# Eleven tiles that outlive a block of a three-block fused kernel

## The chip, the core and the metric

The kernel runs on one core of a Trainium2 chip. The metric is the time of one execution on the device in microseconds. Five engines work from queues of their own: TensorE (PE, its weight loads shown as PEld), VectorE (DVE), ScalarE (ACT), GpSimd (POOL) and SyncE (SP), which here issues all DMA transfers. They are ordered by semaphores alone.

## What is computed

Four layers on x and a context ctx, both 32 x 128 x 512 float32. Their sizes are batch B = 32, T = 128 tokens, D = 512.

```
L0: x = LayerNorm(x + Wo . attention(x Wq, ctx Wk, ctx Wv))       # 32 heads, 8 key/value heads of 16
L1: g, theta = conv(x); phi = conv(ctx); y = softmax(phi theta) g; wy = Wz y + bz
    x = x + gamma * (wy - mean) / sqrt(var + eps) + beta           # mean and var over batch and features
L2: a recurrent mixing layer (32 heads of 16, state from ctx) and its feed-forward part
L3: x = x + cproj(attention(LN(x) q_w, ctx k_w, ctx v_w))          # 16 heads of 32, masked
    x = x + proj(gelu(fc(LN(x))))                                  # 512 -> 2048 -> 512
```

The statistics of L1 run over the whole batch, so L2 can't begin for any row before L1 is done for all.

## The kernel before

`program` runs four functions one after the other, each with tiles, semaphores and an `nc.Block()` of its own. A block ends when all five engines have ended their programs in it.

- `phase_a` (tiles a_...): L0 and the part of L1 up to wy, in 16 turns of two batch rows. It leaves x (`dram["x1"]`), wy (`dram["wy"]`) and the transposed context (`dram["cT"]`) in DRAM.
- `phase_norm` (n_...): the statistics of L1, a few tiny operations that end in the tile `norm`.
- `phase_b` (b_...): L2 in 16 turns of two batch rows. In the idle places of its first and last turns it also computes L3's keys and values for all eight groups of four rows (`unit`, matmuls on L1338 for a K unit and L1343 for a V unit; results through L1492 and L1684 to `dram["k"]` and `dram["v"]`). The units of groups 0 to 2 are side 0 (first turns), the others side 1 (last turns). Their weights and contexts lie in tiles that are not otherwise in use then: for side 0, k_w in `Wfk`, v_w in `Wfr`, the context of even groups in `Wfv` and of odd groups in `Wo`. The result of the layer goes to `dram["x4"]`.
- `phase_c` (c_...): L3 in eight turns of four rows.

Within a block every engine runs the same hand-written table of steps, three static turns ahead of and four behind a loop in a and b (one ahead, one behind in c). SyncE's program is a list of waits and transfers in order; a transfer behind a wait on SyncE can't be issued until that wait is over. Where a step does not exist in a static turn, the engines count its semaphores up instead.

How the blocks begin:

- `phase_b`, SyncE, L1076 to L1096: `vec`, `ident`, `heads`, `parity`, `state` (these five count into `loaded_w`); then `x1g` and `wyg`, the rows of x and wy for the first turn (L1033, L1034, `y_loaded`); then `load_kv(0)` (L1052): k_w, the two halves of group 0's context, v_w, `rows_c` (the bias of v), the halves of group 1's context; then two small states and the weights of L2.
- `phase_b`, TensorE waits for `loaded_w` and for `consts` to reach 6 (L1163), then begins the first units, which wait for `kv_weights` and `groups_loaded`. VectorE waits for `loaded_w`, then sets half, A, two v_pad and heads_wide and copies heads (L1499 to L1505, six counts of `consts`). GpSimd builds its masks, then waits for `consts`. ScalarE normalises wy (L1373), GpSimd adds x (L1709), VectorE takes statistics (L1511).
- `phase_c`, SyncE, L1953 to L1964: four loads of x rows, `ident`, `vec`, q_w, `load_k`, `load_mask`, `load_v`, `rows` (two biases), cproj_w, fc_w (4 MB), proj_w (4 MB). `loaded_k` counts ident and vec, `loaded_att` q_w, rows and cproj_w.
- `phase_c`: VectorE takes the statistics of four rows (L2106 to L2111), GpSimd the reciprocal roots (L2184), VectorE whitens (L2115), and TensorE transposes (L1994), then q (L2000), scores (L2024) and so on. GpSimd's program begins with a wait for the whole of `loaded_att` (L2180); TensorE's and ScalarE's with a wait for `loaded_k`.

How they end: in `phase_a` SyncE's last two turns store the last rows (L334, L338) and wait for them; in `phase_b` the last unit is stored (L1066), then the last two rows (L1044), and SyncE waits for all.

Of the kernel before, what the change touches and what calls it, by code (L numbers as in the profile page):

```python
# [19 lines left out]
P = 128  # L20
# [120 lines left out]
def phase_a(nc, dram, stats):  # L141
# [34 lines left out]
    with ExitStack() as ctx:  # L176
# [44 lines left out]
        cT_stored = sig("cT_stored", 16)  # L221
# [63 lines left out]
        def _(sp):  # L285
# [101 lines left out]
            sp.wait_ge(*cT_stored(N - 1, 16))  # L387
# [335 lines left out]
def phase_b(nc, dram, norm):  # L723
# [89 lines left out]
    with ExitStack() as ctx:  # L813
# [13 lines left out]
        vec = sb("vec", [P, dram["vecs"].shape[1]])  # L827
        ident, heads, parity = sb("ident", [P, P]), sb("heads", [P, HC]), sb("parity", [P, 2])
# [8 lines left out]
        x1g, wyg, x2 = sb("x1g", [P, G, D]), sb("wyg", [P, G, D]), sb("x2", [P, G, D])  # L837
# [85 lines left out]
        def groups_loaded(side, group):  # L923
            nth, buffer = divmod(group - sides[side][0][3][1], 2)
            return kv_context[buffer].sem, 32 * (nth + 1 + (len(range(buffer, NEARLY, 2)) if side else 0))
# [82 lines left out]
        def _(sp):  # L1008
# [43 lines left out]
            def load_kv(side):  # L1052
# [5 lines left out]
                load_group(side, first + 1)  # L1058

# [19 lines left out]
            load(Turn(None))  # L1079
            load_kv(0)  # L1080
# [71 lines left out]
            load_kv(1)  # L1152
            for n in LATE:
                mixed(n)
            turn(Turn(None, add=N + 1), 1, True)
            for slot in kv_stored:
                sp.wait_ge(slot.sem, slot.seen)
            sp.wait_ge(*stored.all(Turn(None, add=N - 1)))

        @block.tensor  # L1160
        def _(pe):
# [166 lines left out]
            def unit(at, name, side, n):  # L1328
# [4 lines left out]
                pe.wait_ge(kv_weights[kind].sem, (16 if kind == "K" else 32) * (side + 1))  # L1333
                pe.wait_ge(*groups_loaded(side, group))
# [162 lines left out]
        def _(dve):  # L1497
# [179 lines left out]
            def unit(at, name, side, n):  # L1677
# [4 lines left out]
                if kind == "V":  # L1682
                    dve.wait_ge(kv_weights["V"].sem, 32 * (side + 1))
# [104 lines left out]
def phase_c(nc, dram):  # L1788
# [25 lines left out]
    with ExitStack() as ctx:  # L1814
# [9 lines left out]
        W = {n: sb(n, [P, KC, D]) for n in ("q_w", "cproj_w")}  # L1824
        fc_w, proj_w = sb("fc_w", [P, KC, 4 * D]), sb("proj_w", [P, FC, D])
        vec = sb("vec", [P, dram["vecs"].shape[1] - VEC0])
        rows, ident = sb("rows", [P, 2 * D]), sb("ident", [P, P])
        cproj_b, proj_b = (rows[:, i * D:i * D + D] for i in range(2))
        half, ones = sb("half", [P, 1]), sb("ones", [P, HD])
        x, res, c_xn = sb("x", [P, G, D]), sb("res", [P, G, D]), sb("c_xn", [P, G, D])  # L1830
# [469 lines left out]
```

## Time and profile before

| | us |
|---|---|
| median of 3 runs | 4326.74 (4323.17 to 4335.41) |
| the profiled execution | 4340.87 |
| its span, from first to last instruction | 4339.1 |
| TensorE busy | 4059.7 (94%) |
| VectorE busy | 2311.0 (53%) |
| ScalarE busy | 1501.9 (35%) |
| GpSimd busy | 1418.6 (33%) |

The span of the profiled execution is cut into 40 slices; each digit is the busy share of an engine in tenths, PEclk is the clock granted to TensorE, in tenths of full speed:

```profile
PE   6999999995999999999999999995999999999998
PEclk8999999997999999999999999997999999999999
DMA  3222122213210010000000001114010110110100
```

The two slices in which TensorE is half busy, the tenth and the twenty-eighth, hold the ends of block a and of block b.

### The profile page before, as it was taken

How to read it: one execution, taken by the hardware profiler on the slowest of the kernel's cores; microseconds unless marked ns; L12 is line 12 of the kernel's file. 1: busy time of each engine (PE TensorE's matmuls, PEld its weight loads, DVE VectorE, ACT ScalarE, POOL GpSimd, SP SyncE). 2: the span in 40 equal slices, each digit the busy share in tenths (PEclk: the TensorE clock that was granted, in tenths of full speed). 3: DMA queues.
4: the chain of work that ended last, by engine and by line, in shares of the span. 5: the costliest groups of instructions: out<-in, count | busy, mean ns of one | idle time of the engine just before them, and what ended most of it. 6: DMA issues, size and time to landing. Idle time of an engine off the chain costs nothing. (4 is left out here: it accounts for less than half of the span.)

```text
span 4339.1 us, 80247 instructions
## 1 busy us (share of the span) xinstructions
PE 4059.7 (94%) x31072; PEld 2547.5 (59%) x31072; DVE 2311.0 (53%) x2657; ACT 1501.9 (35%) x2622; POOL 1418.6 (33%) x1181
## 2 busy tenths in 40 slices
PE   6999999995999999999999999995999999999998
PEld 5666666663666666666666667653445445445443
DVE  4666666662367776766677775325434434334420
ACT  2545555553233344333333443211312222222220
POOL 2433333431254455544455544102211211211210
PEclk8999999997999999999999999997999999999999
DMA  3222122213210010000000001114010110110100
GB/s 111 67 77 77 65 78 70 76 51 105 92 70 26 26 37 26 26 26 26 26 28 31 33 26 57 66 66 158 10 40 1 40 40 1 40 40 1 40 10 10
DMA packets 121397, 205.91 MB, mean 47 GB/s; under 512 B 18993, under 2 KB 39601, under 8 KB 119537
## 3 DMA queue, kind: packets, MB, share of 16 engines
q1 hardware_dynamic: 121072, 200.90, 13.3%
q8 instruction: 287, 4.70, 0.5%
q14 instruction: 38, 0.30, 0.0%
HBM read 125.34 MB, written 67.11 MB: 44 GB/s over the span
## 5 line engine op out<-in xcount | busy, mean ns | idle before, releaser
L1598 DVE COPY_PREDICATED b_A<-b_mask,b_pS 128x2048 f32<-128x2048 uint32 x128 | 458.6, 3583 | 191.5 <-PE b_pS L1287 190.6
L2000 PE MATMUL c_pR<-c_xT,c_fc_w 128*128 128x512 f32 x1024 | 458.6, 599 | 11.7 <-issue 7.7
L2060 PE MATMUL c_pR<-c_proj_w,c_fcT 128*128 128x512 f32 x1024 | 460.0, 598 | 7.2 <-PEq L1899 3.2
L704 POOL TENSOR_TENSOR a_S<-a_S,a_negmax 128x2048 f32<-128x2048 f32 x64 | 230.9, 3608 | 489.7 <-DVE a_negmax L638 489.7
L1762 POOL TENSOR_TENSOR b_R<-b_R,b_Wh 128x512 f32<-128x512 f32 x192 | 228.3, 1189 | 388.3 <-PE b_pS L1287 387.9
L2000 PEld LDWEIGHTS c_pR<-c_xT,c_fc_w 128*128 128x128 f32 x1024 | 192.3, 191 | 251.5 <-issue 246.9
L2060 PEld LDWEIGHTS c_pR<-c_proj_w,c_fcT 128*128 128x128 f32 x1024 | 189.6, 190 | 234.8 <-issue 223.6
L2172 DVE TENSOR_TENSOR c_res<-c_res,c_pR 128x512 f32<-128x512 f32 x128 | 88.1, 688 | 416.0 <-PE c_pR L2060 391.1
L1287 PE MATMUL b_pS<-b_R,b_kT 32*128 32x128 f32 x7168 | 264.2, 283 | 43.8 <-ACT b_A L1445 30.5
L1287 PEld LDWEIGHTS b_pS<-b_R,b_kT 32*128 32x128 f32 x7168 | 221.7, 185 | 139.4 <-issue 101.5
L2071 ACT ACTIVATE c_fcT<-c_pR,c_vec 128x512 f32<-128x512 f32 x128 | 87.9, 687 | 615.7 <-PE c_pR L2000 586.9
L2199 POOL TENSOR_TENSOR c_S<-c_S,c_negmax 128x1024 f32<-128x1024 f32 x64 | 121.3, 1895 | 531.8 <-DVE c_negmax L2144 531.8
L1717 POOL TENSOR_TENSOR b_xm<-b_xm,b_xT 128x512 f32<-128x512 f32 x160 | 207.4, 1321 | 85.9 <-DVE b_xm L1575 85.6
L634 DVE SCALAR_TENSOR_TENSOR a_S<-a_pS,a_mask 128x2048 f32<-128x2048 f32 x64 | 146.3, 2285 | 142.4 <-PE a_pS L419 142.3
L1445 ACT ACTIVATE b_A<-b_pS 16x512 f32<-16x512 f32 (+2 forms) x224 | 199.1, 889 | 50.3 <-PE b_pS L1287 48.8
L552 ACT ACTIVATE a_probsT<-a_pR 128x512 f32<-128x512 f32 x256 | 138.5, 601 | 206.2 <-PE a_pR L428 205.6
L2152 DVE RECIPROCAL c_rec<-c_pR 128x256 f32<-128x256 f32 x64 | 112.5, 1757 | 160.2 <-PE c_pR L2046 153.9
L654 DVE RECIPROCAL a_rec<-a_pR 128x256 f32<-128x256 f32 x64 | 112.5, 1758 | 124.2 <-PE a_pR L443 119.3
L2184 POOL TENSOR_TENSOR c_rstd<-c_veps,c_half 128x1 f32<-128x1 f32 x64 | 40.9, 646 | 395.8 <-DVE c_veps L2111 373.8
L1762 POOL TENSOR_TENSOR b_R<-b_R,b_wT 128x512 f32<-128x512 f32 x32 | 48.2, 1506 | 333.8 <-PE b_pS L1287 333.8
L428 PEld LDWEIGHTS a_pR<-a_ident,a_S 128*128 128x128 f32 x1024 | 118.9, 146 | 59.9 <-issue 59.3
L1172 PE MATMUL b_pR<-b_xm,b_wWr 128*128 128x256 f32 x512 | 137.9, 430 | 12.6 <-POOL b_xm L1717 12.6
(256 smaller groups left out, 7914.8 us busy)
## 6 DMA issues: line engine op xcount, KB each, us to landing
a_c<-ctx SPq DMA_DIRECT2D x16, 512.0 KB, 3.7
a_x<-x SPq DMA_DIRECT2D x16, 512.0 KB, 4.7
a_kexp<-a_kT SPq DMA_DIRECT2D x512, 16.0 KB, 1.8
mid_cT<-a_cT SPq DMA_DIRECT2D x16, 512.0 KB, 2.7
a_xl<-x SPq DMA_DIRECT2D x32, 256.0 KB, 2.7
a_cl<-ctx SPq DMA_DIRECT2D x32, 256.0 KB, 3.0
mid_x<-a_xl SPq DMA_DIRECT2D x32, 256.0 KB, 3.2
mid_wy<-a_wy SPq DMA_DIRECT2D x32, 256.0 KB, 2.1
```

Of the source, the lines that this page charges most:

```text
L552: nc.scalar.activation(probsT[n % 2][:, at:at + 4, :], bank.rearrange("p (h t) -> p h t", h=4), ACT.Exp).then_inc(*emptied["act"].up())
L634: nc.vector.scalar_tensor_tensor(out=S[n % 2][:, :, :], in0=pS[:, :, :].rearrange("p r (h t) -> p (r h) t", t=T), scalar=float(HD) ** -0.5 ...
L704: nc.gpsimd.tensor_tensor(S[n % 2][:, :, :], S[n % 2][:, :, :], negmax[n % 2][:, :].unsqueeze(2).to_broadcast([P, RH, T]), ALU.add)\
L1172: mm = nc.tensor.matmul(bank[:, m * TOK:m * TOK + TOK], w[:, c, at:at + P], src[:, c, :], start=(c == 0), stop=(c == KC - 1))
L1287: mm = nc.tensor.matmul(pS[:, r, c * P:c * P + P].rearrange("p (e n h) -> p e n h", e=2, h=h), kT[par][at, c, g * T:g * T + T], later, sta ...
L1445: ins = nc.scalar.activation(A[rows, :, 2 * h * b + h:2 * h * b + 2 * h], pS[rows, :, :].rearrange("p r (q t) -> p (r q) t", t=T // 2)[:, ...
L1598: nc.vector.copy_predicated(A[:, :, :].rearrange("p q (n two h) -> p q n two h", two=2, h=h)[:, :, :, 1, :], masks[h][:, :].bitcast(U32).r ...
L1717: nc.gpsimd.tensor_tensor(part, part, xT[0][:, 2 * h:2 * h + 2, :, 1:T + 1].rearrange("p k g t -> p (k g) t"), ALU.add)\
L1762: nc.gpsimd.tensor_tensor(later, later, decay, ALU.mult).then_inc(*r_moved.up())
L2000: mm = nc.tensor.matmul(bank, w[:, c, at * P:at * P + P], src[:, c, :], start=(c == 0), stop=(c == KC - 1))
L2060: mm = nc.tensor.matmul(bank, fcT[part % 2][:, m, g * T:g * T + T], proj_w[:, KC * part + m, :], start=(m == 0), stop=(m == KC - 1))
L2199: nc.gpsimd.tensor_tensor(S[n % 2][:, :, :], S[n % 2][:, :, :], negmax[n % 2][:, :].unsqueeze(2).to_broadcast([P, UH, T]), ALU.add)\
```

## The change

Eleven tiles are allocated in `program` instead of in the blocks and handed to them in a dictionary `kept`: `Wfk`, `Wfr`, `Wfv`, `x1g` and `wyg` ahead of block a, `Wk`, `Wr`, `Wv`, `Wg`, `ident` and `vec` behind it. Block c uses `Wg` for q_w, `Wv` for x, `Wk` for kT, `Wr` for v_tm, `wyg` for the bias rows, and `Wfk`, `Wfr`, `Wfv`, `x1g` for xT1, xT2, attT and qT.

- SyncE in block a gets `load_kept`, in the turn after the last row's own, behind one store: it waits for three earlier stores and issues what was at the head of block b: x1g, wyg, k_w, group 0's context, v_w. The wait at the block's end includes them.
- SyncE in block b begins with the same five small loads and then the v bias and group 1's context; instead of loading x1g and wyg it counts `y_loaded` up. For side 0, units wait neither for k_w and v_w nor for group 0.
- SyncE in block b gets `load_last_block`: once all units are stored and the last one's matmuls are done, it loads the first four rows of x, q_w, the first k and v and the two bias rows; behind it stands the last turn's store of the last two rows.
- SyncE in block c counts `x_loaded`, `k_loaded` and `v_loaded` up and issues mask, cproj_w, fc_w, proj_w. `loaded_att` now counts cproj_w alone, and TensorE waits for it at step "o"; the waits for `loaded_k` and GpSimd's for `loaded_att` are gone.

```diff
@@ phase_a, SyncE
+            def load_kept():
+                wait(cT_stored(N - 1, 16))
+                wait(wy_stored[0](N - 2, 16))
+                wait(wy_stored[1](N - 3, 16))
+                for tile, name in (("x1g", "x1"), ("wyg", "wy")):
+                    sp.dma_start(kept[tile][:, :, :], dram[name].rearrange("b t d -> t b d")[:, 0:G, :]).then_inc(*kept_loaded.up(16))
+                sp.dma_start(kept["Wfk"][:, :, :], dram["L3_xattn_k_w"].rearrange("(k p) n -> p k n", p=P)).then_inc(*kept_loaded.up(16))
+                for h in range(2):
+                    sp.dma_start(kept["Wfv"][:, :, h * TOK:h * TOK + TOK], dram["cT"][h, :, :, :]).then_inc(*kept_loaded.up(16))
+                sp.dma_start(kept["Wfr"][:, :, :], dram["L3_xattn_v_w"].rearrange("(k p) n -> p k n", p=P)).then_inc(*kept_loaded.up(16))
...
                 if has(i + -1):
                     store_x1(i + -1, 0)
+                if static and i.add == N:
+                    load_kept()
...
-            sp.wait_ge(*cT_stored(N - 1, 16))
+            sp.wait_ge(kept_loaded.sem, kept_loaded.seen)
@@ phase_b
-        W = {n: sb("w" + n, [P, KC, D]) for n in ("Wk", "Wv", "Wr", "Wg", "Wo", "Wfk", "Wfr", "Wfv")}
+        W = {n: kept[n] if n in kept else sb("w" + n, [P, KC, D]) for n in ("Wk", "Wv", "Wr", "Wg", "Wo", "Wfk", "Wfr", "Wfv")}
-        x1g, wyg, x2 = sb("x1g", [P, G, D]), sb("wyg", [P, G, D]), sb("x2", [P, G, D])
+        x1g, wyg, x2 = kept["x1g"], kept["wyg"], sb("x2", [P, G, D])
@@ phase_b, SyncE
+            def load_last_block():
+                last, name, _, _ = sides[1][-1]
+                wait(R_.filled(Turn(None, add=last + 1), R_.at[name] + 1))
+                for tile, src in ((W["Wv"], dram["x4"][0:GC, :, :].rearrange("b t d -> t b d")), (W["Wg"], dram["L3_xattn_q_w"].rearrange("(k p) n -> p k n", p=P)),
+                                  (W["Wk"], dram["k"][0, :, :, :]), (W["Wr"], dram["v"][0:GC, :, :].rearrange("b t d -> t b d")),
+                                  (wyg, dram["rows_c"][:, D:].rearrange("p (g d) -> p g d", g=2))):
+                    sp.dma_start(tile[:, :, :], src).then_inc(*kv_weights["K"].up(16))
...
-            load(Turn(None))
-            load_kv(0)
+            sp.sem_inc(*y_loaded.up(32))
+            sp.dma_start(kv_rows[0], dram["rows_c"][:, 0:D]).then_inc(*kv_weights["V"].up(16))
+            load_group(0, 1)
             load_state(Turn(None), 0)
...
-            turn(Turn(None, add=N + 1), 1, True)
             for slot in kv_stored:
                 sp.wait_ge(slot.sem, slot.seen)
+            load_last_block()
+            turn(Turn(None, add=N + 1), 1, True)
+            sp.wait_ge(kv_weights["K"].sem, kv_weights["K"].seen)
             sp.wait_ge(*stored.all(Turn(None, add=N - 1)))
@@ phase_b, TensorE, unit
-                pe.wait_ge(kv_weights[kind].sem, (16 if kind == "K" else 32) * (side + 1))
-                pe.wait_ge(*groups_loaded(side, group))
+                if side:
+                    pe.wait_ge(kv_weights[kind].sem, 16 if kind == "K" else 48)
+                if groups_loaded(side, group)[1]:
+                    pe.wait_ge(*groups_loaded(side, group))
@@ phase_c
-            for g in range(G):
-                load_rows(Turn(None), g)
-            sp.dma_start(ident[:, :], dram["ident"]).then_inc(*loaded_k.up(16))
-            sp.dma_start(vec[:, :], dram["vecs"][:, VEC0:]).then_inc(*loaded_k.up(16))
-            weight(loaded_att, W["q_w"], "q_w")
-            load_k(Turn(None))
+            for ready in x_loaded + [k_loaded, v_loaded]:
+                sp.sem_inc(*ready.up(16))
             load_mask(Turn(None))
-            load_v(Turn(None))
-            sp.dma_start(rows[:, :], dram["rows_c"][:, D:]).then_inc(*loaded_att.up(16))
             weight(loaded_att, W["cproj_w"], "cproj_w")
...
@@ phase_c, TensorE
-            pe.wait_ge(loaded_k.sem, loaded_k.seen)
...
-                    pe.wait_ge(loaded_att.sem, loaded_att.seen)
                     linear(j, s, W["q_w"], n, xT1, "n1")
...
                 elif s[0] == "o":
+                    pe.wait_ge(loaded_att.sem, loaded_att.seen)
@@ phase_c, ScalarE
-            act.wait_ge(loaded_k.sem, loaded_k.seen)
@@ phase_c, GpSimd
-            pool.wait_ge(loaded_att.sem, loaded_att.seen)
```

## Rows read from the trace of the kernel before

**Rows 1.** The page, part 1: busy us, share, instructions.

```profile
PE 4059.7 (94%) x31072; PEld 2547.5 (59%) x31072; DVE 2311.0 (53%) x2657; ACT 1501.9 (35%) x2622; POOL 1418.6 (33%) x1181
```

**Rows 2.** TensorE's waits: line, releaser, us in total, times, longest.

```profile
PE c_pR L1994 <- DVE c_c_xn L2115: 43.4, 9, 31.2
...
PE b_pR L1343 <- DMA b_x<-rows_c: 27.2, 1, 27.2
```

**Rows 3.** Timeline, seam one: start, duration, engine, line, op [idle before <- releaser].

```profile
1057.25 0.06 DVE L1499 MEMSET b_half<- 128x1 f32 x1 [7.39 <-DMA b_state<-state_rows]
...
1064.88 0.17 DVE L1505 COPY b_heads_wide<-b_heads 128x8 f32<-128x8 f32 x1
1065.13 2.48 POOL L1709 TENSOR_TENSOR b_wyg<-b_wyg,b_x1g 128x512 f32<-128x512 f32 x2 [10.29 <-DVE b_heads_wide L1505]
...
1070.85 9.71 PE L1343 MATMUL b_pR<-b_wWfr,b_wWfv 128*128 128x512 f32 x16 [27.19 <-DMA b_x<-rows_c]
```

**Rows 4.** Timeline, seam two and block c's first turn.

```profile
2923.32 7.03 PE L1185 MATMUL b_pR<-b_wWfv,b_xT 128*128 128x512 f32 x16
...
2936.46 0.06 DVE L2102 MEMSET c_half<- 128x1 f32 x1 [4.59 <-PEq L813]
2937.99 1.76 SPq L1925 DMA_DIRECT2D c_x<-mid_x  x4
...
2940.76 0.69 DVE L2106 BATCH_NORM_STATS2 c_bn<-c_x 128x6 f32<-128x512 f32 x1 [4.24 <-DMA c_x<-mid_x]
...
2945.35 0.15 DVE L2111 TENSOR_SCALAR c_veps<-c_mv 128x1 f32<-128x1 f32 x1
...
2958.50 2.40 POOL L2184 TENSOR_TENSOR c_rstd<-c_veps,c_half 128x1 f32<-128x1 f32 x4 [21.98 <-DMA c_cproj_w<-L_xattn_cproj_w]
2959.09 2.40 DVE L2115 TENSOR_SCALAR c_c_xn<-c_x,c_mv,c_rstd 128x512 f32<-128x512 f32 x4 [13.58 <-POOL c_rstd L2184]
...
2961.54 3.68 PE L1994 MATMUL c_pR<-c_ident,c_c_xn 128*128 128x128 f32 x16 [31.19 <-DVE c_c_xn L2115]
...
2966.18 5.81 PE L2000 MATMUL c_pR<-c_xT,c_q_w 128*128 128x512 f32 x8 [0.96 <-ACT c_xT L2071]
...
2972.25 3.67 PE L2000 MATMUL c_pR<-c_xT,c_q_w 128*128 128x512 f32 x8 [0.26 <-issue]
...
3045.07 15.51 PE L2000 MATMUL c_pR<-c_xT,c_fc_w 128*128 128x512 f32 x31 [0.87 <-ACT c_xT L2071]
```

**Rows 5.** Windows: us, busy PE PEld DVE ACT POOL, granted clock, DMA share, GB/s.

```profile
1078.00:1090.00 12.00, 12.00 (x51) 9.45 (x51) 3.34 (x9) 1.38 (x2) 0.71 (x1) 1.00 1.06 378
...
2934.00:2938.00 4.00, 0.00 (x0) 0.00 (x0) 0.06 (x1) 0.00 (x0) 0.12 (x1) 0.50 0.00 0
2938.00:2961.00 23.00, 0.00 (x0) 0.00 (x0) 5.54 (x16) 0.00 (x0) 2.40 (x4) 0.50 0.97 355
2961.00:2966.00 5.00, 3.68 (x16) 3.28 (x16) 4.97 (x3) 3.08 (x4) 4.43 (x1) 0.50 1.00 414
...
2982.00:2986.00 4.00, 4.00 (x30) 3.23 (x28) 1.61 (x2) 1.79 (x3) 1.48 (x1) 0.50 0.02 4
```

**Rows 6.** Timeline of SyncE, ends of blocks a and b.

```profile
986.59 0.34 SPq L338 DMA_DIRECT2D mid_wy<-a_wy  x1
...
1011.33 0.33 SPq L338 DMA_DIRECT2D mid_wy<-a_wy  x1
...
2899.94 3.77 SPq L1066 DMA_DIRECT2D mid_v<-b_sx  x2
2928.54 3.75 SPq L1044 DMA_DIRECT2D mid_x<-b_x  x2
```

**Rows 7.** The page, part 6: DMA, count, KB each, median us to landing.

```profile
mid_wy<-a_wy SPq DMA_DIRECT2D x32, 256.0 KB, 2.1
```

**Rows 8.** One matmul line of b, operand in two tiles: min/median/max ns.

```profile
L1338 PE MATMUL b_pR<-b_wWfv,b_wWfk x128: 378/380/380, 1080.4 to 1166.8; 128*128 128x256 f32 x128
...
L1338 PE MATMUL b_pR<-b_wWo,b_wWfk x64: 378/380/483, 1094.2 to 1140.0; 128*128 128x256 f32 x64
```

More of the change, by code:

```diff
@@ L924, in groups_loaded @@
             nth, buffer = divmod(group - sides[side][0][3][1], 2)
-            return kv_context[buffer].sem, 32 * (nth + 1 + (len(range(buffer, NEARLY, 2)) if side else 0))
+            return kv_context[buffer].sem, 32 * (nth + 1 - (buffer == 0) + (len(range(buffer, NEARLY, 2)) if side else 0))
         def stores(slot, side, n):
@@ L1050, in load_group, with load_kv @@
                     sp.dma_start(half_of(side, group, h), dram["cT"][2 * group + h, :, :, :]).then_inc(*kv_context[(group - sides[side][0][3][1]) % 2].up(16))
-            def load_kv(side):
+            def load_kv():
+                side = 1
                 sp.dma_start(kv_k[side][:, :, :], dram["L3_xattn_k_w"].rearrange("(k p) n -> p k n", p=P)).then_inc(*kv_weights["K"].up(16))
@@ L1682, in unit @@
                 if kind == "V":
-                    dve.wait_ge(kv_weights["V"].sem, 32 * (side + 1))
+                    dve.wait_ge(kv_weights["V"].sem, 48 if side else 16)
                     nc.vector.tensor_tensor(dst, bank, kv_rows[side], ALU.add).then_inc(*R_.emptied["dve"].up())
@@ L1785, in phase_b, with phase_c @@
         assert not wrong, wrong
-def phase_c(nc, dram):
+def phase_c(nc, dram, kept):
     NH, HD = 16, 32
@@ L1822, in pair @@
             return [sb(name + str(i), shape) for i in range(2)]
-        W = {n: sb(n, [P, KC, D]) for n in ("q_w", "cproj_w")}
+        W = {"q_w": kept["Wg"], "cproj_w": sb("cproj_w", [P, KC, D])}
         fc_w, proj_w = sb("fc_w", [P, KC, 4 * D]), sb("proj_w", [P, FC, D])
-        vec = sb("vec", [P, dram["vecs"].shape[1] - VEC0])
-        rows, ident = sb("rows", [P, 2 * D]), sb("ident", [P, P])
+        vec, ident = kept["vec"], kept["ident"]
+        rows = kept["wyg"][:, :, :].rearrange("p g d -> p (g d)")
         cproj_b, proj_b = (rows[:, i * D:i * D + D] for i in range(2))
         half, ones = sb("half", [P, 1]), sb("ones", [P, HD])
-        x, res, c_xn = sb("x", [P, G, D]), sb("res", [P, G, D]), sb("c_xn", [P, G, D])
-        xT1, xT2, attT, kT, qT = sb("xT1", [P, KC, TOK]), sb("xT2", [P, KC, TOK]), sb("attT", [P, KC, TOK]), sb("kT", [P, KC, TOK]), sb("qT", [P, 2, TOK])
-        v_tm = sb("v_tm", [P, G, D])
+        x, res, c_xn = kept["Wv"], sb("res", [P, G, D]), sb("c_xn", [P, G, D])
+        xT1, xT2, attT, kT, qT, v_tm = (kept[n] for n in ("Wfk", "Wfr", "Wfv", "Wk", "x1g", "Wr"))
         S, probsT, fcT = pair("S", [P, UH, T]), pair("probsT", [P, UH, T]), pair("fcT", [P, KC, TOK])
@@ L2248, in program, with tiles @@
             dram[n] = nc.dram_tensor("mid_" + n, shape, F32, kind="Internal").ap()
-        phase_a(nc, dram, stats)
+        def tiles(names, shape):
+            return {n: ctx.enter_context(nc.sbuf_tensor("s_" + n, shape, F32)) for n in names}
+        kept = {**tiles(("Wfk", "Wfr", "Wfv"), [P, KC, D]), **tiles(("x1g", "wyg"), [P, 2, D])}
+        phase_a(nc, dram, stats, kept)
+        kept.update({**tiles(("Wk", "Wr", "Wv", "Wg"), [P, KC, D]), **tiles(("ident",), [P, P]), **tiles(("vec",), [P, dram["vecs"].shape[1]])})
         phase_norm(nc, dram, stats, norm)
-        phase_b(nc, dram, norm)
-        phase_c(nc, dram)
+        phase_b(nc, dram, norm, kept)
+        phase_c(nc, dram, kept)
 def _layout(inputs):
```

15 lines of the change are left out of this document (7 added, 8 removed).

## The prediction, made before the changed kernel was run

> **What bounds the kernel now.** I read the busy shares first: TensorE is busy for 94% of the span [rows 1], so outside the stretches in which it stands still nothing that this change touches can help. Next come TensorE's waits, longest first [rows 2]: two single waits stand out, 31.2 us (the longest of the nine on L1994) and 27.2 us (one, on L1343). The timeline puts them at the two seams between the three blocks, and in each seam the reader should look for what ended last.
>
> Seam one, between block a and block b [rows 3]: VectorE waits until 1057.25 for the last of the five small loads (`loaded_w`), then does five memsets and a copy, which ends at 1064.88 + 0.17 = 1065.05; GpSimd, which waits for the same count (`consts` at 6), starts 0.08 us later, at 1065.13. TensorE waits for both signals too, but starts only at 1070.85: its first unit needs `kv_weights` V, and the wait is put down to the load of `rows_c`, seventh behind x1, wy, the K weight, two context halves and the V weight.
>
> Seam two, between b and c [rows 4]: TensorE's last matmuls of b end at 2923.32 + 7.03 = 2930.35. Block c starts at 2936.46, SyncE spends 1.53 us on 27 semaphore increments and issues the first rows at 2937.99. VectorE starts its statistics at 2940.76 and has the last variance at 2945.35 + 0.15 = 2945.50. Then nothing computes for 13 us: GpSimd, which owes the reciprocal root, has a wait at the head of its program for `loaded_att` (q_w, the bias rows and cproj_w, behind 3 MB of other loads), and starts at 2958.50. VectorE whitens from 2959.09 to 2961.49, TensorE starts at 2961.54.
>
> **The change, part by part.** *Seam one.* For the first units PE no longer waits for `kv_weights` or a context; `loaded_w` and `consts` stay in its way, with their five loads still first in the queue. So TensorE starts 0.1 us behind 1065.05, at 1065.15: a gain of 1070.85 - 1065.15 = 5.7 us. Next late is not a transfer but VectorE's memsets, which the diff leaves alone. `rows_c` (256 KB) is now sixth instead of twelfth and is needed only by VectorE's first drain, some 6 us after TensorE's start. The affine of wy on ScalarE comes earlier, but the sum of x1 and wy on GpSimd waits for `consts`, at 1065.13 as before, so that chain neither gains nor bounds. From 1078 on TensorE is busy 12.00 us of 12 [rows 5], so what its start gains is carried on. The block's other weights are queued behind 4 MB less and come sooner.
>
> *What seam one costs in block a.* `load_kept` adds six transfers (x1, wy, the K weight, two context halves, the V weight: 0.5 + 0.5 + 1 + 1 + 1 = 4 MB). It stands in SyncE's program behind an x1 store that directly follows the wy store of 986.59 [rows 6], and waits for three stores, of which that wy store is the latest; it lands, by the median of its kind, 2.1 us later [rows 7]: so at about 989. Behind it in SyncE's queue stand a wy store and an x1 store, issued from 1011.33 [rows 6], so SyncE has 22 us to issue six transfers. No engine of block a waits for a load any more. At 355 to 378 GB/s, which seam two's rows and seam one's show [rows 5], 4 MB take 11 to 12 us, done by about 1001. Cost: nothing. The cover is these 22 us; if it were gone, each further us would hold the stores, and the block's end only if it were more than the 10 us from 1001 to 1011.
>
> Those stores run on the same queue. The Trainium skill ("DMA: Bandwidth & Descriptors", HWDGE ordering) says that each DMA engine consumes its descriptors in ring order, so a small store issued behind megabytes has to let them pass; this speaks against hoisting loads in front of stores. By it a store issued at 989 would land some 11 us late, and the sum would lose that much of seam one; the store issued at 1011.33 meets an empty ring and the sum stays.
>
> *Seam two.* The first rows, k, v, q_w and the two bias rows are there when block c starts, ident and vec as well, and the wait at the head of GpSimd's program is gone. The four `x_loaded` and two other increments come after the same 27: 2937.99 + 0.06 for the first. VectorE starts at 2938.1. From its first statistic to its last variance it takes 2945.50 - 2940.76 = 4.74 us as before, to 2942.85. GpSimd takes 0.60 us for each root (2.40 for four) and the four variances come about 1.1 us apart, so it keeps up; its last root is ready at 2943.5. VectorE whitens four times 0.60 us from 2942.9 on, to 2945.3; the fourth does not have to wait. TensorE starts at 2945.35: a gain of 2961.54 - 2945.35 = 16.2 us. Next late is VectorE's chain of statistics. Block c's mask is the first transfer in its queue now, and is read only after the whitening; its two other weights follow. The first matmul on fc_w comes at 3045.07 [rows 4], 29 us after even the slowest landing that I can make for them (9 MB from 2938.5 at 355 GB/s: 2964; the first use moves to 3029, which leaves 65). No cost.
>
> *What seam two costs in block b.* `load_last_block` waits for the stores of all units (last two issued from 2899.94, the second by about 2903.7 [rows 6], landed some 2 us later, as [rows 7]) and issues 4.5 MB at about 2906: 13 us, done by 2919. The final two stores, which it now precedes on SyncE, come at 2928.54 and later. The wait at the block's end for its count is long satisfied. Cost nothing, with 9 us of cover.
>
> *The clock.* At both seams TensorE works at half rate at first: granted 0.50 where c starts [rows 5], and 8 matmuls that take 3.67 us warm took 5.81 [rows 4]. Seam two stays idle for 15 us instead of 31, seam one for 21 instead of 27; before, 4 us of idling (2930.35 to 2934) were already enough that 0.50 stood from 2934 on [rows 5], so I keep the cold start in the sum. What I can't see is how long it lasts from a moved start, nor whether the second dip at 2982 [rows 5] stays. I bound it by what the rows show: all of it warm would give back about 2 us for the q matmuls, 1 for the transposes and 3 for the dip, a second such lot would cost as much: -6 to +6. I take 0, the middle, since both starts have the same sort of idling ahead.
>
> **The sum.** 5.7 + 16.2 = 21.9 us. The profiled execution had a span of 4339.1 us and took 4340.87; it would become 4317.2 and 4319.0. The median of the runs is 14.1 us under the profiled time, so 4326.74 - 21.9 = **4304.8 us**, or 0.51% less. No engine has anything added inside a loop.
>
> **The rivals.**
> 1. *Seam one doesn't pay* (4326.74 - 16.2 = 4310.5): TensorE starts at 1065 but the first units' drains, or the count of free banks, give the 5.7 us back. For it: VectorE and GpSimd have chains of their own there. Against: TensorE is gapless from 1078, as said.
> 2. *Seam two doesn't pay* (4326.74 - 5.7 = 4321.0): another wait takes the place of GpSimd's. It would have to be one at the head of an engine's program; the loads that remain in block c have none in the first 60 us but the mask, which is small and first.
> 3. *The loads don't land early* (4326.7): the waits added on SyncE hold them until the block's end. It decides at the blocks' ends: 2936.46 for b and after 1011.33 for a, against 2919 and 1001 above.
> 4. *Slower, by placement*: eleven tiles lie elsewhere and push block a's own by 32 KB per partition. If reading and writing them there cost more, it would be charged on every instruction: 0.5% (3 ns of a 592 ns matmul) eats the whole gain, 1% gives 4326.7 + 43.3 - 21.9 = 4348. Against: the same matmul line with its operand in two different tiles has the same 380 ns in both [rows 8].
>
> A rule that bears on that: the Trainium skill ("SBUF — State Buffer") says that DMA and engine accesses use separate ports and can't slow each other. By it the 8.5 MB moved beneath running work are free. No row here times one instruction with and without traffic, so this is only cited; if it were wrong, the moved loads would cost a part of 24 us of TensorE work.
>
> **How the numbers follow.** Forecast 0.80, with its own range of 21.9 give or take 6 and 3 us for the baseline's spread (4323.17 to 4335.41 in three runs): 4296 to 4314. Rival 1: 0.07; rival 2: 0.05; rival 3: 0.04; rival 4: 0.04. The range, 4296 to 4316, holds the forecast and rival 1 and leaves out the rest. A measurement of this kernel can tell 0.3% from no change, that is 13 us: the forecast and most of rival 1 lie beyond it (0.85), rivals 2 and 3 and the forecast's poor end within (0.11), rival 4 on the other side (0.04).
>
> **What the profile after would show.** TensorE's wait at the first L1343 matmul ends with VectorE's copy or memsets and no DMA, about 21.5 us long; the wait on L1994 for the whitening is about 15 us long; from the last matmul of b to c's first transpose 15.0 us instead of 31.2. SyncE's timeline shows six loads at 989 to 995 and five at 2906 to 2912, and the stores at 1011 and 2928 where they were. The groups of the three loops keep their mean durations. The prediction is wrong if a load is issued in the last 10 us of a block, if GpSimd's roots come more than 5 us after block c begins plus 1.6, or if those means move by more than 0.3%.

## The result, and the profile after

The changed kernel took 4312.39 us (median of 5 runs, 4296.15 to 4316.48) against 4326.74 before (now 5 runs, 4323.17 to 4335.41): a ratio of 0.9949, 95% interval 0.9934 to 0.9964, so 15 to 29 us less. The ratio and its interval rest on all runs; the two medians alone are 14.4 us apart. The forecast was 4304.8, or 0.9949 of the median before: the measured median is 7.6 us above it, and the ratio meets it. Timed twice more beside the variants below, the change came out at 0.9969 (0.9956 to 0.9982) and 0.9950 (0.9935 to 0.9965). The profiled execution of the changed kernel had a span of 4310.6 us.

The page of the changed kernel, part 1 and three lines of part 2:

```profile
PE 4053.6 (94%) x31072; PEld 2542.3 (59%) x31072; DVE 2311.7 (54%) x2657; ACT 1502.0 (35%) x2622; POOL 1419.0 (33%) x1181
...
PE   6999999996999999999999999996999999999998
...
PEclk9999999998999999999999999998999999999999
```

The engines do what they did [rows 1]; the two half-empty slices are slices of 0.6 now. TensorE's waits in the changed kernel, in order of their sum:

```profile
PE b_pS L1313 <- ACT b_A L1473: 30.7, 41, 1.1
PE c_pR L2013 <- DVE c_c_xn L2133: 26.5, 9, 14.3
...
PE b_pR L1371 <- DVE b_heads_wide L1533: 21.4, 1, 21.4
```

Both long single waits of [rows 2] are shorter, 31.2 to 14.3 us and 27.2 to 21.4, and the second has another releaser: VectorE's copy to heads_wide instead of the DMA of rows_c. The first seam in the timeline of the changed kernel, first SyncE at the end of block a, then the start of b:

```profile
990.72 0.34 SPq L338 DMA_DIRECT2D mid_wy<-a_wy  x1
991.17 0.37 SPq L334 DMA_DIRECT2D mid_x<-a_xl  x1
992.89 0.39 SPq L346 DMA_DIRECT2D s_x1g<-mid_x  x1
...
996.00 2.58 SPq L350 DMA_DIRECT2D s_Wfr<-L_xattn_v_w  x1
1015.90 0.36 SPq L338 DMA_DIRECT2D mid_wy<-a_wy  x1
...
1066.69 0.17 DVE L1533 COPY b_heads_wide<-b_heads 128x8 f32<-128x8 f32 x1
1066.94 2.48 POOL L1737 TENSOR_TENSOR s_wyg<-s_wyg,s_x1g 128x512 f32<-128x512 f32 x2 [10.25 <-DVE b_heads_wide L1533]
1066.96 9.44 PE L1371 MATMUL b_pR<-s_Wfr,s_Wfv 128*128 128x512 f32 x16 [21.42 <-DVE b_heads_wide L1533]
```

The moved loads are issued within 5.7 us, 17 us ahead of the next store; GpSimd and TensorE start side by side, 0.1 us behind VectorE's copy. Set beside [rows 3], where TensorE came 5.7 us after GpSimd, that is the gain of this seam. The second seam:

```profile
2894.08 0.39 SPq L1081 DMA_DIRECT2D s_Wv<-mid_x  x1
...
2917.17 3.77 SPq L1057 DMA_DIRECT2D mid_x<-b_x  x2
...
2925.08 0.06 DVE L2120 MEMSET c_half<- 128x1 f32 x1 [4.59 <-PEq L827]
2926.61 0.69 DVE L2124 BATCH_NORM_STATS2 c_bn<-s_Wv 128x6 f32<-128x512 f32 x1 [1.47 <-SPq L1981]
...
2931.27 1.91 DVE L2133 TENSOR_SCALAR c_c_xn<-s_Wv,c_mv,c_rstd 128x512 f32<-128x512 f32 x4
...
2933.23 3.67 PE L2013 MATMUL c_pR<-s_ident,c_c_xn 128*128 128x128 f32 x16 [14.27 <-DVE c_c_xn L2133]
```

VectorE's first statistic is released by SyncE's increment and no transfer, 1.53 us after the block begins (4.30 in [rows 4]); whitening follows at once; TensorE starts 8.2 us after the block begins instead of 25.1.

The spans of the two profiled executions differ by 28.5 us, more than their idle times at the seams (5.8 + 16.9 = 22.7). The rest is not the change's: it lies in the loops of a and b, and the experiments show how far that varies.

### The profile page after: what moved, and what is told of

It reads as the page before. It is cut to its first block and busy times, and to the rows that moved or that the text cites. A ratio compares the mean times of both kernels' runs of the same rounds, so it can differ in the third digit from the quotient of the medians.

```text
span 4310.6 us, 80239 instructions
## 1 busy us (share of the span) xinstructions
PE 4053.6 (94%) x31072; PEld 2542.3 (59%) x31072; DVE 2311.7 (54%) x2657; ACT 1502.0 (35%) x2622; POOL 1419.0 (33%) x1181
## 5 line engine op out<-in xcount | busy, mean ns | idle before, releaser
L2019 PE MATMUL c_pR<-s_Wfr,c_fc_w 128*128 128x512 f32 x1024 | 461.8, 602 | 9.4 <-issue 5.4
L2019 PEld LDWEIGHTS c_pR<-s_Wfr,c_fc_w 128*128 128x128 f32 x1024 | 193.5, 192 | 250.7 <-issue 246.0
L2089 ACT ACTIVATE c_fcT<-c_pR,s_vec 128x512 f32<-128x512 f32 x128 | 87.9, 687 | 616.0 <-PE c_pR L2019 587.2
L652 DVE TENSOR_REDUCE a_negmax<-a_S 128x16 f32<-128x2048 f32 x64 | 146.3, 2286 | 2.2
```

The source lines that it names most:

```text
L652: nc.vector.tensor_reduce(negmax[n % 2][:, :], S[n % 2][:, :, :], AX.X, ALU.max, negate=True).then_inc(*max_found.up())
L2019: mm = nc.tensor.matmul(bank, w[:, c, at * P:at * P + P], src[:, c, :], start=(c == 0), stop=(c == KC - 1))
```

## The experiments

Each was read in two ways: the two idle times of TensorE from its trace (between the last matmul of one block and the first of the next), and the ratio of its timed runs to those of the kernel before on the same chip. The first repeats within 0.1 us in the three traces of the changed kernel and within 1.3 us in the two of the kernel before; the second is known to 5 to 8 us.

**Seam one alone.**

```diff
-            load_last_block()                     # and SyncE's wait for it
-            for ready in x_loaded + [k_loaded, v_loaded]:
-                sp.sem_inc(*ready.up(16))
+            for g in range(G):
+                load_rows(Turn(None), g)
+            weight(loaded_q, W["q_w"], "q_w")     # then k, mask, v, rows
...
+            pool.wait_ge(loaded_att.sem, loaded_att.seen)
+            pool.wait_ge(loaded_q.sem, loaded_q.seen)
```

> The changed kernel with its second seam undone: block c loads its first rows, q_w, k, v and bias rows itself again, GpSimd waits at its head for q_w, the bias rows and cproj_w, and load_last_block is gone; ident and vec stay kept. Theory (two additive seams): TensorE's idle time between a and b is 21.4 us, between b and c 30 to 31 us; time 5.8 us under the kernel before, a ratio near 0.9987. Rival (placement costs or gives something by itself): a ratio that differs from that by over 0.2% either way. Rival (seam one's gain is given back inside block b): the first loop turn of b starts no earlier after the first unit than before, ratio 1.000.

Measured: idle 21.5 and 29.05 us, ratio 0.9995 (0.9982 to 1.0008). The first idle time is as forecast, the second 1 us under its range. The ratio tells neither the 0.9987 of the theory nor 1.000 apart, so this seam rests on the trace. Of the rivals, that the gain is given back inside block b falls by the trace: from the last matmul of a to the fourth save of x in b (the line that stores `wyg`, once a turn) it takes 324.6 us, in the kernel before 329.9 (323.6 to 324.6 in the four traces with this seam as changed, 328.0 to 330.3 in the six without it, the kernel before among them). The timed gain, 2 us, is smaller than the idle time removed. That alone would be noise, but it begins a series that is taken up below.

**Seam two alone.**

```diff
-                if static and i.add == N:
-                    load_kept()
...
-            sp.sem_inc(*y_loaded.up(32))
+            load(Turn(None))
+            load_kv(0)
```

> The changed kernel with its first seam undone: load_kept is gone, block b loads x1g, wyg, k_w, group 0 and v_w itself and its units wait for them. Theory: idle time between a and b 27.2 us, between b and c 14.3 us; time 16.9 us under the kernel before, ratio 0.9961. Rival (part of the gain at seam two is lost later in block c): the time from c's first transpose to the end is over 1378 us. With seam one alone it should add up to the whole change (0.9949).

Measured: idle 27.1 and 14.3 us, ratio 0.9968 (0.9957 to 0.9979), with the 0.9961 of the theory inside. From c's first transpose to the end it took 1373.8 us, so nothing is lost there. The two seams are independent: each has the idle time alone that it has in the whole change, within 0.1 us.

**The places alone**, both edits above together, twice.

> The changed kernel with both seams undone: only the places of the tiles in SBUF differ from the kernel before, and ident and vec aren't loaded again in c. Theory: ratio 1.000 within 0.1%, mean durations of each matmul, VectorE and GpSimd group as before, idle 27.2 and 30 to 31 us. Rival (the places account for part of the 28.5 us by which the profiled executions differ, above all for the 7.5 us inside block b): ratio 0.998 or less, or 1.002 or more.

> Places alone, a second time. Removed idle time: 2.4 us (ident and vec are not loaded again), so 0.9994 if the places cost nothing; the first measurement was 1.0006 (0.9991 to 1.0020). Theory (places are free): 0.9994 within its interval. Rival (the places cost some 5 us over the whole kernel): 1.0006 again, with an interval that excludes 0.9994.

Measured: 1.0006 (0.9991 to 1.0020) and 1.0016 (1.0005 to 1.0027); idle 27.0 and 29.0 us, then 27.0 and 29.8. The second interval excludes both 1.000 and the 0.9994 of the expectation, so the sharper form of "places are free" falls. But TensorE's instructions are not slower by it: its busy time in these two traces is 4049.2 and 4056.0 us, in the two of the kernel before (the second is the next run) 4059.7 and 4046.1. One shape of matmul in three traces, min/median/max ns (kernel before, places alone, places alone again):

```profile
L1194 PE MATMUL b_pR<-b_ident,b_xn x256: 272/273/332, 1097.7 to 2895.4; 128*128 128x128 f32 x128
```

```profile
L1214 PE MATMUL b_pR<-s_ident,b_xn x256: 272/273/329, 1096.4 to 2890.1; 128*128 128x128 f32 x128
```

```profile
L1214 PE MATMUL b_pR<-s_ident,b_xn x256: 272/273/329, 1095.3 to 2891.9; 128*128 128x128 f32 x128
```

**The kernel before as a variant.**

> The kernel before, submitted as if it were a variant. Theory: ratio 1.000 within 0.12%, so that the intervals of the others can be trusted; in its trace idle times 27.2 and 31.2 us, and the rest of its span (without the two idle times) within 4262 to 4281 us, as in the ten traces so far. If it differs from itself by 0.2% or more, the shortfalls seen so far (variants came out 0.4 to 12 us less fast than the removed idle time says) mean nothing.

Measured: 0.9994 (0.9983 to 1.0005), idle 27.0 and 29.9 us. The kernel before doesn't differ from itself, so the comparison is sound to 0.1%. The second idle time is news: it was 31.2 in the first profile of the same kernel. Its first transpose, in the timeline of this second trace:

```profile
2952.55 3.61 PE L1994 MATMUL c_pR<-c_ident,c_c_xn 128*128 128x128 f32 x16 [29.94 <-DVE c_c_xn L2115]
```

GpSimd waits there for the last of several megabytes, and when that lands varies by a us. Over the two traces the kernel before idles for 27.1 + 30.6 = 57.7 us, the changed kernel over its three for 21.4 + 14.2 = 35.7 (35.6 to 35.7 in each). The change removes 22.0 us of idle time.

**The wait split, no load moved.** Made from the kernel before:

```diff
@@ phase_c, GpSimd
             pool.wait_ge(consts.sem, 1)
-            pool.wait_ge(loaded_att.sem, loaded_att.seen)
...
                     pool.wait_ge(*whitened(j, G))
+                    pool.wait_ge(loaded_att.sem, loaded_att.seen)
                     nc.gpsimd.tensor_tensor(x[:, :, :], x[:, :, :], cproj_b ...
@@ SyncE and TensorE
-            weight(loaded_att, W["q_w"], "q_w")
+            weight(loaded_q, W["q_w"], "q_w")     # loaded_q is waited for at q, loaded_att at o
```

> The kernel before with no load moved: GpSimd's wait for q_w, bias rows and cproj_w goes from the head of its program in c to its first use of a bias row, and q_w counts on a semaphore of its own, which alone holds TensorE's q step; cproj_w is waited for at step o. Theory (seam two was a wait in the wrong place more than late loads): whitening follows the statistics at about 2945.6, TensorE's first transpose comes at about 2948 instead of 2961.5, idle time 17.7 us, time 13.5 us under the kernel before, ratio 0.9969: five sixths of what the moved loads gave at this seam. Rival (the loads themselves are needed): TensorE gets its transposes early, but then waits for q_w or v behind them, so that scores begin less than 5 us sooner, ratio 0.999 or more.

Measured: idle 26.8 and 17.0 us, ratio 0.9972 (0.9961 to 0.9983). In its timeline of seam two:

```profile
2935.81 1.91 DVE L2116 TENSOR_SCALAR c_c_xn<-c_x,c_mv,c_rstd 128x512 f32<-128x512 f32 x4
...
2937.77 3.67 PE L1994 MATMUL c_pR<-c_ident,c_c_xn 128*128 128x128 f32 x16 [17.00 <-DVE c_c_xn L2116]
...
2942.41 6.07 PE L2000 MATMUL c_pR<-c_xT,c_q_w 128*128 128x512 f32 x8 [0.96 <-ACT c_xT L2072]
...
2948.11 4.52 POOL L2197 TENSOR_TENSOR c_x<-c_x,c_rows 128x2048 f32<-128x2048 f32 x1 [11.26 <-DMA c_cproj_w<-L_xattn_cproj_w]
```

TensorE goes from the transposes to q without waiting for q_w, and GpSimd's wait for the late load is beside its path. The rival falls, by the ratio too (0.999 was its figure). Three edited waits bring 13.6 of the 16.4 us (30.6 less 17.0 or 14.2) that the second seam gives. Of these, GpSimd's wait, moved off the head of its program, lets TensorE transpose early; the semaphore of its own for q_w lets q follow. Seam two was a wait in the wrong place; the five moved loads add the last 2.8 us, which is the landing of the first rows.

**The units ahead of the memsets**, on top of the change.

```diff
@@ phase_b, TensorE
-            pe.wait_ge(loaded_w.sem, loaded_w.seen)
-            pe.wait_ge(consts.sem, 6)
...
                 if s == "n1":
+                    if i.reg is None and i.add == 0:
+                        pe.wait_ge(loaded_w.sem, loaded_w.seen)
+                        pe.wait_ge(consts.sem, 6)
```

> The changed kernel, with TensorE's wait for loaded_w and for consts (VectorE's memsets) moved from the head of its program in b to its first step that needs them, n1. Theory (the memsets are what ended last): the first unit starts once SyncE has counted the semaphores up, near 1.5 to 3 us after block b begins, so 10 to 12 us sooner after the last matmul of a (idle 10 us instead of 21.4); the first four units fill four banks before any is drained, 17 us at the lower clock, so the drains at about the old time hold nothing; ratio to the kernel before 0.9922. Rival (the drains bound the units): TensorE starts sooner but waits for the third or fifth bank, and n1 comes less than 4 us sooner, ratio 0.994.

Measured: idle 9.3 and 14.2 us, ratio 0.9949 (0.9930 to 0.9967). The start of b:

```profile
1054.03 8.67 PE L1372 MATMUL b_pR<-s_Wfr,s_Wfv 128*128 128x512 f32 x16 [9.30 <-SPq L1024]
1062.53 13.98 PE L1367 MATMUL b_pR<-s_Wfv,s_Wfk 128*128 128x256 f32 x64
1076.34 3.62 PE L1367 MATMUL b_pR<-b_wWo,s_Wfk 128*128 128x256 f32 x16
1079.80 1.04 PE L1218 MATMUL b_pR<-s_ident,b_xn 128*128 128x128 f32 x8
1080.67 3.60 PE L1372 MATMUL b_pR<-s_Wfr,s_Wfv 128*128 128x512 f32 x8
1086.75 2.66 PE L1236 MATMUL b_pR<-b_xn,b_w 128*128 128x256 f32 x8 [2.48 <-issue]
```

The memsets were what ended last at seam one: without them TensorE starts 12 us sooner, no drain holds the units, and n1 comes 35.1 us after block a's last matmul instead of 48.0. At the fourth save 11 us of it are left (313.1 against 324.2). So the drains don't bound the units. Yet the timed runs gained no more than the changed kernel's best measurement, and the expected 0.9922 lies outside the interval. That is the plainest case of the shortfall.

**The same, with SyncE's start in another order**, twice.

```diff
@@ phase_b, SyncE
-            for s in signals:
+            # the five small loads first, then:
+            for s in signals[-6:] + signals[:-6]:
@@ phase_c, SyncE
-            for s in signals:
+            for s in first + [s for s in signals if s not in first]:   # first: statistics, roots, whitened, x_loaded
                 sp.sem_inc(s.sem, s.per)
+                if s in x_loaded:
+                    sp.sem_inc(*s.up(16))
```

> As units_first, and SyncE in b issues the five small loads before it counts the semaphores up and counts TensorE's own first; in c it counts first what the statistics wait for, the loaded rows among it. Theory: another 1.5 to 2.9 us at seam one and 1.0 to 1.3 us at seam two, where VectorE's first statistic comes 0.5 us after the block begins instead of 1.5; ratio 0.9913. Rival (the increments overlap with something else that begins as late): no change against units_first.

> The fastest variant, a second time, in the company of the changed kernel. Removed idle time 36.4 us: 0.9916 if nothing is given back; with 5 us given back 0.9927. Either way 0.0025 to 0.0035 under the changed kernel in the same set of runs.

Measured: 0.9934 (0.9917 to 0.9951) and 0.9938 (0.9920 to 0.9955), medians 4295.31 and 4302.97 us; idle 9.05 and 12.95 us both times. It is the fastest version here, but less fast than was expected: 0.9913 lies outside the first interval, 0.9916 outside the second, and it came out 0.0012 under the changed kernel of the same set of runs and not 0.0025 to 0.0035. Seam two gained the 1.3 us that was expected: VectorE's first statistic comes 0.25 us after the block begins.

```profile
2914.02 0.06 DVE L2124 MEMSET c_half<- 128x1 f32 x1 [4.56 <-PEq L827]
2914.27 0.69 DVE L2128 BATCH_NORM_STATS2 c_bn<-s_Wv 128x6 f32<-128x512 f32 x1 [0.19 <-SPq L1936]
```

Seam one gained 0.25 us of the 1.5 to 2.9 expected: the issue of the five loads takes SyncE's first 2.2 us in b, and the increments that TensorE needs, now first of their kind, stand behind it. The two halves of the edit nearly cancel there.

**The moved loads at the end of block a instead.**

```diff
             def store_wy(j, g):
                 wait(out(j, "wy%d" % g))
+                if j.reg is None and j.add == N - 1 and g == 1:
+                    load_kept()
                 sp.dma_start(one(dram["wy"], j, g), wy[g][:, :]).then_inc(*wy_stored[g].up(16))
```

> The changed kernel with load_kept moved to the last place of block a: behind the wait for the last wy result, ahead of its store. Theory (4 MB take 11 to 12 us wherever nothing covers them, and a store issued behind them on the same queue lands behind them): the last store lands some 8 us after its issue instead of 2, block a ends 12 us later, and the idle time between a and b is 33 us, 6 us more than in the kernel before. Rival (transfers run side by side and a small store passes the large loads): the store lands in about 2 us; the block's end then waits for the loads alone. If the moved loads were not covered in the changed kernel either, this one would not be slower than it.

Measured, in one execution of 4310.18 us: idle 34.6 us at seam one, 7.5 more than in the kernel before. SyncE's last transfer of block a, and its waits (engine, line, waited for, us in total, times, longest):

```profile
1042.64 1.78 SPq L352 DMA_DIRECT2D s_Wfr<-L_xattn_v_w  x1
1044.46 1.32 SPq L340 DMA_DIRECT2D mid_wy<-a_wy  x1
```

```profile
SPq L404 <- DMA mid_wy<-a_wy: 9.0, 1, 9.0
```

The store lands 10.4 us after its issue, where the same line's median in the changed kernel is 2.1: it lands behind the loads. So 4 MB do cost 13 us of idle time where nothing covers them (34.6 against 21.4), and the cover was real. At the fourth save in b the 13 us are still there (337.6 us after block a's last matmul, 324.2 in the changed kernel). The whole execution does not show them: its 4310.18 us lie among the 4312.39, 4307.43 and 4310.57 of the changed kernel's three profiled ones, since outside the two idle times it took 4259.5 us, the least of all traces. This version ran once, and differences of this size between executions are the subject of the next section.

**The change a second and third time.**

> The changed kernel as it is, timed again beside the variants. Theory (two seams, 5.8 and 16.9 us): ratio 0.9948; both idle times as in its first profile (21.4 and 14.3 us), while the span of block b between them need not be 7.5 us shorter than before again: if that was chance, it lies anywhere within some 10 us of 1859. Rival (the 7.5 us belong to the change): block b again takes 1850 to 1854 us.

> The changed kernel, a third time, since its two ratios (0.9949 and 0.9969) hardly overlap. Removed idle time 22.7 us: 0.9948 if nothing is given back. Rival (some 5 us given back, by places or otherwise): 0.9960, with an interval that excludes 0.9948.

Measured: 0.9969 (which excludes 0.9948) and 0.9950, as said; the interval of the third holds both the 0.9948 and the 0.9960 that it was to tell apart, so it doesn't decide. Idle 21.4 and 21.5 us at seam one, 14.2 at seam two in both. Block b took 1858.9 and 1858.8 us between its first and last matmul, against 1852.0 in the first profile and 1859.5 and 1860.2 in the two of the kernel before. So the 7.5 us by which b was shorter in the first pair was chance and no part of the change.

## Where the rest of the time goes: the granted clock

Without its two idle times, the span was between 4259.5 and 4280.7 us in fourteen traces, with no order by the idle time removed: 4280.7 and 4267.5 for the kernel before, 4274.9, 4270.1 and 4273.1 for the changed one. Windows over two successive turns of block c in the changed kernel show what varies (us, busy time of PE, PEld, DVE, ACT, POOL, granted clock, DMA share, GB/s). The head of a turn that took 165.0 us from store to store, and that of the next, which took 169.4:

```profile
3171.00:3186.00 15.00, 13.76 (x45) 6.82 (x44) 2.52 (x4) 4.07 (x5) 3.80 (x3) 1.00 0.58 209
3186.00:3201.00 15.00, 15.00 (x48) 7.59 (x47) 10.83 (x18) 5.42 (x8) 8.11 (x6) 1.00 0.25 75
```

```profile
3336.00:3351.00 15.00, 11.44 (x39) 5.48 (x37) 2.52 (x4) 4.07 (x5) 2.55 (x2) 1.00 0.58 208
3351.00:3366.00 15.00, 14.86 (x31) 6.59 (x32) 10.89 (x18) 2.06 (x3) 9.28 (x7) 0.89 0.27 79
```

The turns run the same program. In the second, TensorE stands for 2.46 us more at the head, and in the window behind that the granted clock is at its lower level for 3.4 us; with both the turn is 4.4 us longer. The wait comes first, and a turn can have it without the dip. Nothing that the timeline shows ends it ("issue"), but the DMA view of 3336 to 3352 has packets of the kind "instruction" there, of which 3171 to 3187 has none:

```profile
3351.14 2.33 PE L2019 MATMUL c_pR<-s_Wfr,c_fc_w 128*128 128x512 f32 x3 [2.46 <-issue]
```

```profile
q8 instruction: 2, 0.03, 1.5%
```

The fourteen traces have 84 such turns of c, the first six from store to store in each. The 34 in which no or one packet of instructions is loaded took 164.8 to 165.0 us, the 50 with eight to ten of them 165.0 to 169.4. The wait at the head was 1.99 us or more in fifteen of the 50; seven of these have a dip of 3.4 us behind it and took 169.0 to 169.4, eight have none and took 167.2 to 167.7. So in block c turns are longer with loads of instructions, and longer still with a dip behind one. All 84 turns fit this, though no run here changed those loads alone, so it is read from the traces and not shown by an experiment. The kernel before has eight to ten of these packets in all six turns of both its traces, the changed kernel in two or three, and the run with the loads last in none, which is a part of its luck.

Over the whole execution the clock weighs more. For each trace: how long the granted clock was at its lower level outside the two idle times, TensorE's busy time, and its idle time outside the two seams:

| | lower level, us | busy, us | other idle, us |
|---|---|---|---|
| kernel before, two traces | 157.5, 111.7 | 4059.7, 4046.1 | 221.0, 221.3 |
| the change, three traces | 136.5, 139.9, 150.2 | 4053.6, 4052.7, 4055.2 | 221.3, 217.4, 217.9 |
| units first | 176.3 | 4067.6 | 212.6 |
| units and order, twice | 155.2, 131.7 | 4056.1, 4050.6 | 215.5, 216.9 |
| loads last | 119.2 | 4046.0 | 213.4 |

The instructions are the same, and the busy time follows the clock: over all fourteen traces the correlation is 0.97, with 0.33 us more of busy time for each us at the lower level (a fitted line). Busy times differ by up to 21.6 us, the other idle times by up to 8.7. So most of the spread is TensorE working slower, and less of it TensorE waiting longer. The further 12 us of idle time that units first removes went with 13.8 us more of busy time in the one trace of units first (against the mean of the change's three).

The timed runs have a mean granted clock each, rounded to 0.001. A mean lower by 0.001 means 0.002 of the span at half rate, in which TensorE, if it works, falls behind by at most 0.001 of the span, 4.3 us (2.9 us by the line fitted above). Idle time counts as 0.50, so that removing 22 us of it should raise the mean by 22 x 0.5 / 4328 = 0.0025. The table sets the idle time removed, the clock that this would give from the 0.978 of the kernel before, the median of the clocks, and the sum of idle time and clock beside the measured change:

| | idle removed, us | clock expected | median clock | change by both, us | measured, us |
|---|---|---|---|---|---|
| the change, 2nd and 3rd time | 22.0 | 0.9805 | 0.979, 0.979 | -15.5 | -13.4, -21.6 |
| seam one | 7.1 | 0.9788 | 0.9775 | -1.5 | -2.2 |
| seam two | 16.3 | 0.9799 | 0.978 | -8.1 | -13.9 |
| places, twice | 1.7, 0.9 | 0.9781 | 0.977, 0.976 | +3, +8 | +2.6, +6.9 |
| split wait | 13.8 | 0.9796 | 0.9785 | -9.0 | -12.1 |
| units first | 34.1 | 0.9819 | 0.978 | -17 | -22 |
| units and order, twice | 35.7 | 0.9821 | 0.9805, 0.9795 | -29, -24 | -28.6, -26.8 |

Measured is the ratio's distance from 1 times the median of the kernel before in the same runs. Idle time alone overstates the gain in every row (only in the change's first timing was it met, with 22.1 us), by 6 us on average and 12 at most; with the clock the sum misses by 3 on average and 6 at most, mostly by charging too much; with 2.9 us in place of 4.3 it misses by 2 on average and 4 at most. So the shortfall goes with TensorE running at its lower rate in more of the loops. By the mean ratios it is 8 us for the fastest version and 6 for the places alone, which their intervals tell from nothing; the 3 us of the change they don't, and its three traces lie within those of the kernel before in their time at the lower level. What brings the dips on is not settled: in block c they stand behind waits for instructions, in a and b what stands ahead of them was not traced. That other places, or an earlier start, shift the small waits of the loops against each other is a guess that no run here tests. The clocks of the timed runs are medians of rounded numbers and the before's own ratio lay 0.06% off 1, so the table supports the account and doesn't prove it; the traces show that the busy time moves with the clock, not why a version gets more dips.

## Why the prediction was right

- **Seam one, 5.7 us.** Measured 5.8, with the releaser that was named. The start came 0.10 us after VectorE's copy, as the sum had it. Rival 1 (drains or banks give it back) is excluded by the fourth save, which comes 324.6 us or less after block a's last matmul with this seam and 328.0 or more without.
- **Seam two, 16.2 us.** Against the same profile 16.9: whitening took 1.91 us, not 2.40, as three roots were ready before it began. Against the mean of two traces of the kernel before it was 16.4. Rival 2 (another wait in its place) did not come up: TensorE's wait ends with VectorE's whitening, as before, and the whitening follows the statistics at once.
- **The moved transfers at no cost.** Right in both blocks: the last matmul of block a ends at 1036.4 to 1045.5 us in the seven traces with the loads where the change has them and at 1035.4 to 1043.7 in the six without. The price that I set on missing cover, 11 to 12 us, was 13.2: the run with the loads last shows a store behind them landing after 10.4 us instead of 2.1. The Trainium skill ("DMA: Bandwidth & Descriptors", HWDGE ordering) says that each DMA engine takes its descriptors in ring order, with which this agrees.
- **Rival 3** (loads land late) is excluded by the rows of both seams: VectorE's copy releases TensorE at the first and SyncE's increment VectorE at the second, and no transfer does.
- **The clock, taken as 0.** The cold start at seam two is that of the first profile before: 0.50 granted for c's transposes and 0.57 while q begins, 0.72 in the dip behind them, and the lower level ends 8.9 us after the first transpose starts in both. The windows of the changed kernel over that stretch:

```profile
2931.00:2937.00 6.00, 3.67 (x16) 3.27 (x16) 5.93 (x8) 2.39 (x4) 4.61 (x2) 0.50 1.04 426
2937.00:2943.00 6.00, 5.22 (x7) 2.23 (x8) 1.18 (x1) 0.72 (x1) 0.90 (x1) 0.57 0.99 411
...
2951.00:2957.00 6.00, 4.34 (x40) 3.62 (x44) 3.11 (x3) 1.75 (x4) 3.50 (x2) 0.72 0.32 117
```

  In the second trace of the kernel before it ended after 3.4 us, in all three of the changed kernel after 8.9. So the term was not sure to be 0: if the longer start belongs to the change, which isn't shown, it takes back half of 5.5 us. And I had looked for the clock's share at the seams only. Most of the spread lies in the loops (20 us between executions); that the sum came within 3 us of the mean of three ratios owes something to luck there.
- **Rival 4** (placement) was put as dearer instructions. That is not so. Its result, a cost that comes with the places alone, was there at 0.16% in the second measurement and not clear of noise at 0.06% in the first; that it comes through the clock is argued from the clocks of the timed runs and not shown.

The mean of the three ratios of the change is 0.9956, 19 us, where the sum gave 21.9; each ratio is known to 6 us, so the two don't differ. That the first ratio is the forecast's to the fourth place is luck, and of the 28.5 us between the two first spans 5.8 are chance. The text called a mean duration that moves by over 0.3% a sign against it; the mean of the fc matmuls moved from 599 to 602 ns (0.5%), while their median was 593 before and 592 after. In the second trace of the kernel before the mean was 598, in the second of the changed one 598 too. That test was too sharp for a mean that mixes the two rates.

## What to carry to other kernels

At a seam between stages, list every wait at the head of every engine's program and what each engine's first instructions really read: here a wait at the head of GpSimd's program, for loads that its first instructions don't read, held the kernel for 14 us, and moving it (with a semaphore of its own for the load that is needed first) brought five sixths of what moving five loads brought. Loads moved ahead of a seam cost nothing here where the queue was empty again before the next store, and 13 us of idle time where it was not. Behind the removed load stood memsets, worth 12 us more of idle time, twice what the load gave, though the timed runs didn't return all of it. Read such a gain from the idle times in the traces and not from single spans, which vary by 20 us here, mostly with the clock.

## What the runs showed of the hardware that I had not expected

- Turns of 165.0 us take 2.2 to 2.7 us longer when TensorE waits 2.0 to 2.5 us at their head, always in turns in which packets of instructions are loaded, and 1.7 us more when the clock dips for 3.4 us behind that.
- In a kernel that keeps TensorE busy 94% of the time its busy time varies by 21.6 us between executions, as much as the whole change gives, and moves with the time at the lower clock level (111.7 to 176.3 us).
- A 256 KB store behind 4 MB of loads on SyncE's queue landed 10.4 us after its issue (2.1 otherwise).
- SyncE's increments of semaphores at a block's start are on the path: 27 take 1.5 us, and moving the ones that matter to the front brought 1.3.
- VectorE's 128x512 multiplication for the mask took 4.63 us in the changed kernel and ended 0.28 us after GpSimd's addition beside it, and 0.43 us in the split version, where GpSimd came later. First the changed kernel, then the split one:

```profile
2933.26 4.64 POOL L2213 TENSOR_TENSOR s_Wv<-s_Wv,s_wyg 128x2048 f32<-128x2048 f32 x1 [0.96 <-DVE c_c_xn L2133]
2933.55 4.63 DVE L2147 TENSOR_SCALAR c_limit<-c_limit 128x512 f32<-128x512 f32 x1
```

```profile
2941.80 0.43 DVE L2130 TENSOR_SCALAR c_limit<-c_limit 128x512 f32<-128x512 f32 x1
```

  TensorE doesn't wait for either in these 4 us. The Trainium skill ("SBUF — State Buffer", on the shared port pair of VectorE and GpSimd) has this as an exclusive lock held for a whole instruction, with which the rows agree.
